# Tokens' stage in another order on two engines, and eleven full products ahead of it on PE

## The reference, cut to what matters

```python
def _layernorm(x, axis=-1, eps=1e-05):
    m = jnp.mean(x, axis=axis, keepdims=True)
    v = jnp.var(x, axis=axis, keepdims=True)
    return (x - m) / jnp.sqrt(v + eps)

# small = ctx (64 rows), large = layernorm(x) (512 tokens)
aa = jnp.sum(a * a, axis=-1)[:, None]
bb = jnp.sum(b * b, axis=-1)[None, :]
D = jnp.sqrt(jnp.maximum(aa + bb - 2.0 * a @ b.T, 0.0))
R[i, j] = D[i, j] + min(R[i-1, j], R[i, j-1], R[i-1, j-1])
# walk back from the last cell; every cell (i, j) of the path adds small[i] to row j
x = x + aligned
x = x + ffn(layernorm(x), w1, b1, w2, b2)     # 256 -> 1024 -> 256, values rounded to 8 bits
```

## Time and profile before

| | us |
|---|---|
| median of 3 runs | 178.85 |
| lowest, highest | 178.79, 178.98 |
| the profiled execution's own time | 178.78 |
| its span | 177.0 |
| what lies around the span | 1.78 |
| busy PE, DVE, ACT, POOL | 115.9, 152.1, 107.8, 40.5 |

### The profile page before, as it was taken

How to read it: one execution, slowest core, us unless ns; L and a number is a source line. 1 busy time by engine, 2 the same in 40 slices (tenths; PEclk the granted TensorE clock), 3 DMA queues, 4 the chain that set the end, 5 groups by cost and what they waited for, 6 DMA issues and landing times.

```text
span 177.0 us, 3519 instructions
## 1 busy us (share of the span) xinstructions
PE 115.9 (65%) x1123; PEld 79.8 (45%) x1123; DVE 152.1 (86%) x732; ACT 107.8 (61%) x203; POOL 40.5 (23%) x101
## 2 busy tenths in 40 slices
PE   6999970000028698000007979999999999999991
PEld 6798960000015473000002435655666666666680
DVE  4899968999999999999999479998898999896361
ACT  3687676699998010053150089878777777878720
POOL 7964896000000000000000000014050413222250
PEclk9999996555555556755555799999999999999999
DMA  5997008400009950020203422005454637282948
GB/s 147 355 349 224 6 0 335 171 0 0 2 4 312 344 175 0 0 74 2 74 3 131 65 41 33 0 0 63 59 62 58 72 52 83 40 98 25 114 50 191
DMA packets 19554, 16.88 MB, mean 95 GB/s; under 512 B 5712, under 2 KB 19152, under 8 KB 19408
## 3 DMA queue, kind: packets, MB, share of 16 engines
q1 hardware_dynamic: 14288, 12.69, 22.5%
q0 software_dynamic: 3808, 3.67, 17.1%
q10 hardware_dynamic: 1440, 0.30, 0.8%
HBM read 7.48 MB, written 9.18 MB: 94 GB/s over the span
## 4 chain that ended last, share of the span: by engine, by line
DVE 40%; PE 38%; POOL 7%; DMA 6%; ACT 3%; issue 2%; SPq 2%; POOLq 0%; DVEq 0%; ACTq 0%
PE y L1381 14%; PE h L1362 9%; DMA X<-in_x_dram 6%; DVE R L913 6%; DVE Y L1139 5%; PE t L1362 5%; PE h L1403 3%; DVE A L885 3%; DVE carry L903 3%; DVE M L904 3%; DVE enter L1122 3%; PE e L1321 3%; POOL lengths L499 3%; DVE bcarry L1121 3%; SPq L356 2%
## 5 line engine op out<-in xcount | busy, mean ns | idle before, releaser
L520 POOL DMA_DIRECT2D out_dram<-E x14 | 17.0, 1217 | 125.7 <-DVE E L1108 125.7
L1381 PE MATMUL y<-w2T,XT 128*128 128x256 bf16 x240 | 35.8, 273 | 0.0
L1381 PEld LDWEIGHTS y<-w2T,XT 128*128 128x128 bf16 x240 | 23.3, 98 | 14.0 <-DVE XT L1052 0.3
L694 ACT ACTIVATE h_int<-h,b_s 128x512 int16<-128x512 f32 x37 | 25.3, 686 | 4.9 <-PE h L1362 4.3
L1403 PE MATMUL h<-w1T 128*128 128x512 bf16 x21 | 8.0, 546 | 23.8 <-DVE enter L1122 23.8
L1362 PE MATMUL h<-M,w1T 128*128 128x512 bf16 x74 | 21.9, 380 | 0.8 <-ACT M L687 0.7
L1301 PE MATMUL t<-ident_bf,w_raw 128*128 128x128 bf16 x32 | 4.6, 311 | 26.9 <-ACT w_raw L628 25.2
L1098 DVE TENSOR_SCALAR XT<-h_int 128x1024 bf16<-128x1024 int16 x28 | 12.1, 440 | 8.2 <-ACT h_int L694 8.2
L1301 PEld LDWEIGHTS t<-ident_bf,w_raw 128*128 128x128 bf16 x32 | 3.1, 147 | 28.4 <-issue 25.5
L1403 PEld LDWEIGHTS h<-w1T 128*128 128x128 bf16 x21 | 2.5, 130 | 28.5 <-DVE enter L1122 24.6
L694 ACT ACTIVATE h_int<-t,b_s 128x512 int16<-128x512 f32 x19 | 13.0, 686 | 3.4 <-PE t L1362 3.2
(11 more groups left out here) (239 smaller groups left out, 304.8 us busy)
## 6 DMA issues: line engine op xcount, KB each, us to landing
X<-in_x_dram SPq DMA_DIRECT2D x8, 512.0 KB, 9.0
out_dram<-E POOLq DMA_DIRECT2D x14, 256.0 KB, 4.3
w_raw<-in_L_ffn_w_dram SPq DMA_DIRECT2D x2, 1024.0 KB, 5.9
out_dram<-b_s SPq DMA_DIRECT2D x2, 1024.0 KB, 5.9
out_dram<-b_s SPq DMA_DIRECT2D x2, 768.0 KB, 9.5
S<-in_ctx_dram SPq DMA_DIRECT2D x1, 512.0 KB, 4.0
out_dram<-E SPq DMA_DIRECT2D x4, 128.0 KB, 3.2
path_dram<-A SPq DMA_DIRECT2D x3, 160.0 KB, 1.8
```

Of the source, the lines that this page charges most:

```text
L520: nc.gpsimd.dma_start(tiles_out[:, b:b + 2, quad_of(g, 2 * h), :], res[:, g % 2, 2 * h:2 * h + 2, :], accum_op=ALU.add).then_inc(out_store ...
L694: nc.scalar.activation(h_int[:, g % 2, n, :], hidden_banks[i % 3][:, :], ACT.Identity, bias=b1_s[:, n:n + 1], scale=1.0 / W_ONE).then_inc( ...
L1381: mm = nc.tensor.matmul(results(g, t, t + 1)[:, 0, :], hq[:, g % 2, n, t * P:t * P + P], w2T[:, n, :], start=(n == 0 and not bias), stop=( ...
```

## The change

On POOL, the memset of E leaves out slots 7 to 31 (so there are two memsets, of 7 x 65 and 8 x 65 elements, and all counts of `pool_const` behind it grow by one), the memsets of `b2_rows` and `ones` go behind the tokens, and the tokens' functions come in another order: `spread_of` 0, 1, then `token_lengths` 0, `spread_of` 2, `token_lengths` 1, `spread_of` 3, `token_lengths` 2 and 3. On DVE, `distances` is cut in two functions (`scaled`, `lengthened`), `first_masks` moves from the second quarter's `bn_stats` to behind `lengthened(1)`, and `scales(1)` and `scales(3)` move. On PE, `LEAD` is 11 in place of 40, and the products are full ones.

```diff
-LEAD = 40
+LEAD = 11
-            nc.gpsimd.memset(E[:, :, :], 0.0).then_inc(pool_const, 1)
+            nc.gpsimd.memset(E[:, 0:CH - 1, :], 0.0).then_inc(pool_const, 1)
+            nc.gpsimd.memset(E[:, HR:SLOTS, :], 0.0).then_inc(pool_const, 1)
...
-            nc.gpsimd.memset(b2_rows[:, :], 0.0).then_inc(pool_const, 1)
-            nc.gpsimd.memset(ones[:, :], 1.0).then_inc(pool_const, 1)
...
-            for k in range(LOADS - 1):
-                spread_of(k)
-            token_lengths(0)
-            spread_of(LOADS - 1)
-            token_lengths(1)
-            token_lengths(2)
+            spread_of(0)
+            spread_of(1)
+            for k in range(LOADS - 2):
+                token_lengths(k)
+                spread_of(k + 2)
+            token_lengths(LOADS - 2)
             token_lengths(LOADS - 1)
+            nc.gpsimd.memset(b2_rows[:, :], 0.0).then_inc(pool_const, 1)
+            nc.gpsimd.memset(ones[:, :], 1.0).then_inc(pool_const, 1)
...
-            def distances(k):
+            def scaled(k):
                 v.wait_ge(prods_made, 3 * k + 1)
                 nc.vector.tensor_tensor(flat(norms[:, k, :, :, :]), flat(turned_back[:, k % 2, :, :, :]), scale_by(k),
                                         ALU.mult).then_inc(prods_made, 1)
+
+            def lengthened(k):
                 v.wait_ge(prods_made, 3 * k + 2)
                 v.wait_ge(lengths_made, 2 * k + 2)
...
             load_moments(0)
-            for j in range(B // 2):
-                moments(1, j)
-            first_masks()
-            for j in range(B // 2, UL):
-                moments(1, j)
+            load_moments(1)
             load_moments(2)
             scales(0)
             load_moments(3)
+            scales(1)
             turned(0)
-            scales(1)
-            distances(0)
+            scaled(0)
+            lengthened(0)
             turned(1)
             scales(2)
-            distances(1)
+            scaled(1)
+            lengthened(1)
+            first_masks()
             turned(2)
+            scaled(2)
             scales(3)
-            distances(2)
+            lengthened(2)
             last_distances(0)
             last_distances(1)
...
-                nc.tensor.matmul(bank5[0:TW, 0:8], ident[:, 0:TW], ident[:, 0:8], start=True, stop=True)
+                nc.tensor.matmul(bank5[:, 0:P], ident[:, :], ident[:, :], start=True, stop=True)
```

More of the change, by code:

```diff
@@ L457, in _ @@
                 nc.gpsimd.memset(shifts[:, i:i + 1], shift).then_inc(shifts_made, 1)
-            pool.wait_ge(pool_const, 2)
+            pool.wait_ge(pool_const, 3)
             nc.gpsimd.memset(bass.AP(E, HR * EW, [[SLOTS * EW, P], [CH, 4], [TW + 1, NC]]), BIG).then_inc(pool_const, 1)
@@ L531, in roots @@
                     nc.scalar.activation(norms[:, k, :, :, :], norms[:, k, :, :, :], ACT.Relu).then_inc(clamped, 1)
-                act.wait_ge(pool_const, 3)
+                act.wait_ge(pool_const, 4)
                 for e in range(2):
@@ L632, in _ @@
             act.wait_ge(b_shift, 4)
-            act.wait_ge(pool_const, 5)
+            act.wait_ge(pool_const, 6)
             nc.scalar.activation(b1_s[:, :], b1_q[:, :], ACT.Identity, bias=shifts[:, 3:4],
@@ L1287, in _ @@
             dots(3)
-            pe.wait_ge(pool_const, 4)
+            pe.wait_ge(pool_const, 5)
             pe.wait_ge(w_clip, 2)
@@ L1384, in output @@
                     mm.then_inc(y_done, 1)
-            pe.wait_ge(pool_const, 6)
+            pe.wait_ge(pool_const, 7)
             pe.wait_ge(b_clip, 2)
```

## The result

The changed kernel takes 179.71 us in the median of five runs (179.55 to 179.84), the kernel before 178.91 (178.79 to 179.15): ratio 1.004, 95% interval 1.0027 to 1.0053. It is slower by 0.8 us, and the interval leaves out no change. The forecast was 179.3, slower.

The account below looks back on a forecast made before the run. The tokens' stage is bound by POOL, and a shift of DVE's first transpose out of E (32.83) passes to the end. 178.78 + 0.55 - 0.05 = 179.28, on the median 179.35, said as 179.3; range 178.6 to 179.9.

Parts of the forecast that it names:

- signs named for being right: Trace signs listed as confirming the prediction; among them, DVE idle for 1.4 us at 12.3.
- the sum: DVE's tokens' stage from 19.49: the last quarter's first addition starts at 30.2, not 29.67, so +0.55.
- POOL's constants: POOL's memsets ahead of the tokens: POOL comes to the tokens 1.7 us sooner, but the gain is nothing.
- The masks' rival: DVE's single-input masks also exclude POOL: 0.3 to 0.6 beyond the forecast, 179.6 to 179.9; chance 0.13.
- the forecast's own case: Masks' 1.57 eats what POOL's new order gives, late scales(3) makes lengths(3) last: 179.0 to 179.6; chance 0.57.
- The no-change case: POOL's two small operations win over lengthened(2), addition at 29.7 to 29.8: 178.9 to 179.0; chance 0.16.
- The faster case: lengths(3) in time, scales(3) done by 26.3, stage ends on DVE's own path: -0.75, 178.1; chance 0.14.
- The lead: PE's eleven full products: 22 records in 4.7 us, clock rise some 3 us sooner, priced at nothing.
- The cover: PE's last dots and SP's weight loads 1.7 later, loads done about 35, ACT reads at 38.25: 3 us stay.
- The correction: PE at 93.94: shifted alignment products may fall behind the clock's rise; at most 0.1 back, taken as 0.05.

Follow-up runs that it names:

- e4_head_alone: The kernel before with only POOL's constants changed (E's memset in two pieces, two memsets behind the tokens): 180.79 us, ratio 1.0099.
- e3_both: The changed kernel with S_r1 waiting for the context lengths and first_masks back among the second quarter's bn_stats: 179.08 us, ratio 1.0011.
- e5_masks_moved: The kernel before with only first_masks moved behind the second quarter's distances: 181.01 us, ratio 1.0103.
- e2_sr1_waits: The changed kernel with POOL's S_r1 waiting for the context lengths, masks where the change put them: 180.55 us, ratio 1.0082.
- e12_masks_in_wait: The changed kernel with first_masks between the last quarter's first scaling and its addition: 180.87 us, ratio 1.0103.
- e9_early_lead: The kernel before with POOL's new order, early reciprocals on DVE and the lead of eleven full products: 177.43 us, ratio 0.9917.

## Why the prediction was right, and where it was off

- **Sign and mechanism held.** The deciding addition was forecast at 30.2 and came at 30.41; a wait of over 1 us ahead of it was forecast and is 1.15. The masks were to stand at 24.4 to 26, and stand at 24.45 to 25.98. The last reciprocal was to come at 27.3, and comes at 27.47. `bb_part` was to be held up to 0.6 or more, and takes 0.73. The experiment that takes both edits back fits that chain: with masks and `S_r1` repaired the last reciprocal is at 25.52 and the addition at 29.40. One of the signs named for being right failed: DVE wasn't idle at 12.3.
- **The size.** +0.50 was forecast against 0.80 measured. Where the sum has +0.55 at the addition, 0.74 was measured. It lacks two things: the `bn_stats` end 0.08 later (below), and a reciprocal that stood between a transpose and its scaling, where it filled the transpose's latency, stands alone now: from the start of `turned(0)` or `scales(1)`, whichever is first, to `scaled(0)` it was 0.87 before (19.49 to 20.36) and is 1.02 (19.57 to 20.59). That is 0.15, and it moves `scales(3)` with it. Together they are about the 0.19 that the sum lacks. The remaining 0.1 to 0.2 lie behind 33.56, and the runs didn't single out a cause: from the addition to the end of the execution the twelve experiments' profiles and the two kernels spread from 149.0 to 150.0.
- **The step that failed** is "POOL's constants": "POOL then comes to the tokens 1.7 us sooner ... The gain is nothing". The prediction looked at what waits for POOL, not at what the moved work would run into. `S_r1` came beside DVE's context lengths, by the very exclusion that the prediction had read from the earlier trace rows, and DVE's tokens began 1.85 us later. In e4_head_alone this costs 1.9 us. In the change it costs 0.08 against the trace of the kernel before (and up to 0.4 against others: the first reciprocal is at 16.67, in e3_both at 16.25), because the late DVE fills the time in which it would have been idle without the masks, 1.3 us by the prediction and 1.53 in e5_masks_moved. Two errors thus cancelled: DVE wasn't idle there, and it was late.
- **Luck in the number.** The run nearest to the kernel that the prediction worked out, in which POOL's constants cost nothing, is e2_sr1_waits, and that one takes 180.55, beyond the range's 179.9, because its masks meet POOL's `lengths`. In its trace the third quarter's tokens were there almost in time and `scales(0)` came at 14.96. In the changed kernel the late DVE gives `scales(0)` only at 16.67, so that POOL's list is later and its `lengths` begin when the masks are nearly done. By these two traces the overlooked stall helped the forecast to come out. The loads land at different times in them, though (DVE waits for none in one, for the last in the other), and no run separates the two.
- **The masks' rival** (given 0.13) was not what happened in this kernel: the masks took 1.53, no more than before. The measured 179.71 lies in that rival's 179.6 to 179.9 and just outside the 179.0 to 179.6 of the forecast's own case, but by the sizes above and not by the rival's way. Its mechanism is true all the same, and its price of 0.3 to 0.6 was low for e2_sr1_waits, 1.25 above the forecast. In e2_sr1_waits, e5_masks_moved and e12_masks_in_wait single-input masks took 0.56, 0.60 and 1.00 us in place of 0.23 to 0.26 while POOL was in `lengths` (in the last case in its memsets too). The traces agree with the second half of the Trainium skill's rule too ("SBUF — State Buffer", "SBUF: two separate sides"), as far as single-input operations are held up; that these ran in a two-port mode no trace here shows. In the changed kernel POOL was in small operations until 25.82.
- **The no-change case** needed POOL's two small operations to get in ahead of `lengthened(2)`. They didn't: `bb_part` started at 27.79, just behind the addition's 27.75, and took 0.73.
- **The faster case** named `scales(3)` by 26.3 as its condition. That isn't enough: e3_both has it at 25.52 and is at no change, because POOL then ends the third quarter's `lengths` only at 26.95 and DVE waits 1.32 us ahead of `lengthened(2)` at 27.08. Only with POOL's list early too is the kernel faster, as in e9_early_lead, with the last reciprocal at 24.74.
- **The lead** was priced rightly in length (4.65 against 4.7) and effect: PE is on the higher clock by 6.55, and the addition doesn't move for it by more than the runs tell. The cover for the late dots and weight loads held too: ACT reads the weights at 38.98 without a wait, 0.73 after where it did.
- **The correction** of 0.05 for the products at 94 us can't be told from the end of the execution, but its mechanism shows: PE did the later ones at the higher clock (4.73 us in place of 6.12; the mean granted clock from 94 to 101 us is 0.73 in place of 0.58), and then waited 1.49 us for the flags' DMA. The alignment began 0.67 later than before (100.84 against 100.17) where the transposes out of E had been 0.73 later, so 0.06 came back there:

```profile
94.62 4.73 PE L1406 MATMUL h<-w1T 128*128 128x512 bf16 x14 [25.15 <-DVE enter L1125]
100.84 0.28 PE L1324 MATMUL e<-S_hi,R 64*128 64x256 bf16 x2 [1.49 <-DMA R<-path_dram]
```

## What to carry to other kernels

Where two engines exclude each other for some operations, an edit that makes one of them sooner has to be read against the other's list at the new time, not only against what waits for it: here 1.7 us less of memsets ahead of a subtraction on POOL cost 1.9. An expectation that holds in the sum may hold by two errors, so the parts have to be looked at too: when a change has several parts, undo them one by one and together, since one part can live in the idle time that another has opened. And a short operation on which another engine's long chain waits (the reciprocals) belongs where its input is ready, even in the middle of a row of longer ones: with POOL's new order that was worth 0.8 and 1.1 us against the kernel before in the two measurements of one kernel, and 1.5 in the two kernels that have the full products as well.

## What the runs showed of the hardware that was not expected

- A DVE operation with two SBUF inputs waits out POOL's subtraction however small it is itself: 1.76 and 2.14 us on 128x4 elements beside a subtraction of 2.12. Beside POOL's memset of E, 2.27 us at 4.80, DVE's same operations took 0.17 and 0.15, and beside POOL's last memsets (30.25 to 30.70 in the changed kernel) its addition at 30.41 took 0.42 as elsewhere: these memsets don't hold up such operations. In e12_masks_in_wait six masks, four of them single-input ones, ended together just behind the same two memsets; what held them isn't shown further.
- Single-input DVE operations in fp32 and from int32 are held up too (0.56 to 1.00 in place of 0.25), `bn_stats`, `STREAM_TRANSPOSE` and `RECIPROCAL` in no trace (in the kernel before, the reciprocal at 25.97 takes 0.21 inside the `lengths` of 25.58 to 26.77).
- With the tiny products PE's granted clock rose at 9.8 to 12.8 us in the six traces that have them, with the full ones at 4.7 to 7.6 in the eight others. The moment isn't fixed to the kernel's start, so it has to be read from each trace.
